# Scores kept and masked in PSUM in natural order, read permuted by the exponential

## The reference

```python
latent_kv = x @ w_kv_down              # 1024 x 128
kv = latent_kv @ w_kv_up               # k and v, 16 heads of 64
q = (x @ w_q)
att = einsum('bqhd,bkhd->bhqk', q, k) * 64 ** -0.5
att = where(causal, att, -inf); att = softmax(att, axis=-1)
y = einsum('bhqk,bkhd->bqhd', att, v) @ w_out
```

## Time and profile before

| | |
|---|---|
| Median of 3 runs | 1843.12 us (1841.56 to 1847.8) |
| The profiled execution, its own time | 1841.02 us |
| Its span | 1839.6 us |
| Busy in the span | TensorE 95%, VectorE 68%, ScalarE 49%, GpSimd 47% |
| Pair loop of the first batch, scores of the first round to the last round's | 29.3 to 235.4 us |
| Granted TensorE clock | 0.995 of full speed |

### The profile page before, as it was taken

How to read it: one execution, slowest core, us unless ns; L and a number is a source line. 1 busy time by engine, 2 the same in 40 slices (tenths; PEclk the granted TensorE clock), 3 DMA queues, 4 the chain that set the end, 5 groups by cost and what they waited for, 6 DMA issues and landing times.

```text
span 1839.6 us, 41212 instructions
## 1 busy us (share of the span) xinstructions
PE 1748.0 (95%) x16374; PEld 1237.8 (67%) x16374; DVE 1259.3 (68%) x2775; ACT 894.8 (49%) x1970; POOL 856.5 (47%) x1282
## 2 busy tenths in 40 slices
PE   7899999998999999999999999999999999999998
PEld 4666775757567677566856777756675666765667
DVE  5688857626788884862678888575367888667445
ACT  5577725133567662422357675332246667443233
POOL 2677753141177784222127777324113777731410
PEclk9899999999999999999999999999999999999999
DMA  8555540141355553032135555204014555420500
GB/s 233 121 138 141 118 149 1 21 72 36 87 133 126 127 125 119 1 54 40 36 107 129 130 125 119 106 1 85 8 37 132 128 125 129 109 92 2 92 1 25
DMA packets 119343, 163.76 MB, mean 89 GB/s; under 512 B 30224, under 2 KB 86256, under 8 KB 118128
## 3 DMA queue, kind: packets, MB, share of 16 engines
q1 hardware_dynamic: 105712, 154.83, 35.1%
q10 hardware_dynamic: 13440, 6.30, 1.2%
HBM read 62.44 MB, written 4.24 MB: 36 GB/s over the span
## 4 chain that ended last, share of the span: by engine, by line
PE 79%; DVE 9%; SPq 5%; ACT 3%; issue 1%; DMA 1%; POOL 1%; DVEq 0%; POOLq 0%
PE bank L661 13%; PE scores L641 12%; PE scores L450 12%; PE bank L450 7%; PE bank L702 5%; SPq L978 3%; PE bank L708 3%; PE bank L704 3%; PE scores L1702 2%; PE scores L1615 2%; PE scores L1086 2%; SPq L347 2%; PE scores L1143 2%; PE scores L421 1%; PE scores L1262 1%; PE bank L718 1%
## 5 line engine op out<-in xcount | busy, mean ns | idle before, releaser
L866 POOL COPY placed<-prob 32x768 f32<-32x768 f32 x384 | 316.4, 824 | 27.5
L287 POOL TENSOR_TENSOR rstd<-rstd,minus_half 128x2 f32<-128x2 f32 x96 | 69.6, 726 | 549.7 <-DVE rstd L286 548.7
L905 ACT ACTIVATE prob<-prob,neg_max 128x768 f32<-128x768 f32 (+5 forms) x384 | 273.6, 714 | 97.0 <-DVE neg_max L787 97.0
L661 PEld LDWEIGHTS bank<-placed,v_t 128*64 128x64 f32 x4608 | 252.2, 138 | 73.5 <-issue 73.5
L661 PE MATMUL bank<-placed,v_t 128*64 128x128 f32 x4608 | 275.3, 276 | 14.9 <-DMA placed<-prob 11.2
L641 PE MATMUL scores<-k_t,q_t 64*128 64x128 f32 (+10 forms) x2176 | 287.9, 410 | 0.0
L795 DVE STREAM_TRANSPOSE prob<-prob 128x1536 f32<-128x1536 f32 x128 | 223.0, 1766 | 21.0 <-ACT prob L905 20.8
L641 PEld LDWEIGHTS scores<-k_t,q_t 64*128 64x128 f32 x2176 | 165.0, 187 | 71.8 <-issue 60.2
L787 DVE CUSTOM_DVE_ANT_1 prob<-scores,hx 128x128 f32<-128x128 f32 (+4 forms) x320 | 165.3, 576 | 46.3 <-PE scores L641 44.4
L854 POOL COPY rec_wide<-rec 128x128 f32<-128x128 f32 x256 | 65.5, 291 | 245.2 <-DVE rec L799 178.3
L866 POOL COPY placed<-hx 32x768 f32<-32x768 f32 x192 | 158.1, 824 | 13.7
(11 more groups left out here) (254 smaller groups left out, 3272.6 us busy)
## 6 DMA issues: line engine op xcount, KB each, us to landing
placed<-prob SPq DMA_DIRECT2D x640, 96.0 KB, 2.2
f<-in_L_ffn_f SPq DMA_DIRECT2D x16, 2048.0 KB, 13.3
placed<-hx SPq DMA_DIRECT2D x320, 96.0 KB, 2.1
x<-in_L_attn_x SPq DMA_DIRECT2D x8, 512.0 KB, 4.4
mod_rows<-mod_scratch SPq DMA_DIRECT2D x32, 128.0 KB, 5.4
out<-x SPq DMA_DIRECT2D x16, 256.0 KB, 2.1
w_ring<-in_L_attn_w_q ACTq DMA_DIRECT2D x24, 128.0 KB, 2.4
w_ring<-in_L_attn_w_kv_up ACTq DMA_DIRECT2D x48, 64.0 KB, 2.1
```

The lines of the kernel that those rows point to most:

```text
L287: step = pool.do(lambda e, ts=ts: nc.gpsimd.tensor_tensor(rstd[:, ts], rstd[:, ts], minus_half[:, ts], op=ALU.pow), var, filled)
L661: last = nc.tensor.matmul(out_bank[rows_, at_:at_ + P], v_t[pair % 2][:, j, rows_], placed[m % 2][:, :, head, first_block(m, i) + j, :], s ...
L866: nc.gpsimd.tensor_copy(placed[m % 2][target * GROUP:(target + 1) * GROUP, source, :, :, :], prob[m % 3][source * GROUP:(source + 1) * GRO ...
L905: nc.scalar.activation(p_, p_, ACT.Exp, scale=-1.0, bias=neg_max[:, k:k + 1], accum_out=row_sum[:, k:k + 1]).then_inc(flow["exp_done"], 1)
```

## The change

Keys, scores and mask are in natural order. The score matmuls are cut at bank edges alone. VectorE masks the scores in place in PSUM, all parts of head 0 first, then those of head 1. The exponential reads PSUM in the permuted order and writes `prob`. An exponential waits for the masks of all parts of its head that have a share in its banks (last_beside), not for its own alone. TensorE's waits for the score banks go by exp_done instead of masked, and the wait for the moves goes from VectorE to ScalarE's first exponential of a round. The masks count per head (part_number), and ScalarE's order of exponentials is head by head too.

```diff
-        future = hx[:, 0:TH, :].rearrange("p t n -> p (t n)").rearrange("p (g m) -> p g m", g=GROUPS)
-        future_edge = future[:, :, (T - 1) * GROUP:]
+        future = hx[:, 0:TH, :].rearrange("p t n -> p (t n)")
+        future_edge = future[:, (T - 1) * P:]
...
-            out=future_edge, in_=future_edge, compare_op=ALU.is_ge, fill=BIG, base=0, pattern=[[-GROUP, GROUPS], [-1, GROUP]],
+            out=future_edge, in_=future_edge, compare_op=ALU.is_ge, fill=BIG, base=0, pattern=[[-1, P]],
...
-            return parts_through(m) - HEADS * (len(tiles_in(m)) - i) + head + 1
+            return parts_through(m) - len(tiles_in(m)) * (HEADS - head) + i + 1
...
         def pieces_of(m, i):
 
-            at_, width, pieces = first_block(m, i) * P, (tiles_in(m)[i] + 1) * GROUP, []
-            for g in range(GROUPS):
...
+            at_, end, key, pieces = first_block(m, i) * P, (first_block(m, i) + tiles_in(m)[i] + 1) * P, 0, []
+            while at_ < end:
+                edge = min(end, (at_ // 512 + 1) * 512)
+                pieces.append((at_, key, key + edge - at_))
+                at_, key = edge, key + edge - at_
             return pieces
+
+        def last_beside(m, i):
+
+            return max(j for j in range(len(tiles_in(m))) if first_block(m, j) // 4 <= last_bank(m, i))
...
+        def scores_of(m, i, head):
+            blocks = blocks_in(m, i)
+            return score_tiles[head][:, :, :].rearrange("p a n -> p (a n)")[:, blocks.start * P:blocks.stop * P]
...
                 if m > 0:
-                    e.wait_ge(flow["masked"], base["masked"] + parts_through(m - 1))
+                    e.wait_ge(flow["exp_done"], base["exp_done"] + parts_through(m - 1))
...
-                        last = nc.tensor.matmul(score_tiles[head][:, at_ // 512, at_ % 512:at_ % 512 + count],
+                        last = nc.tensor.matmul(score_tiles[head][:, at_ // 512, at_ % 512:at_ % 512 + hi - lo],
                                                 q_t[buf][rows_, tile * P:(tile + 1) * P],
-                                                k_of[buf][rows_, groups, lo:hi], start=True, stop=True)
+                                                k_t[buf][rows_, lo:hi], start=True, stop=True)
...
             def turn_inverse(m):
                 e.wait_ge(flow["widened"], base["widened"] + m + 1)
-                e.wait_ge(flow["masked"], base["masked"] + parts_through(min(m + 1, ROUNDS - 1)))
+                e.wait_ge(flow["exp_done"], base["exp_done"] + parts_through(min(m + 1, ROUNDS - 1)))
...
-                nc.vector.tensor_copy(keys_half(0, int(j[1])), by_group(bank_of(0, j))).then_inc(flow["job_read_dve"], 1)
+                nc.vector.tensor_copy(k_t[0][:, int(j[1]) * HW:(int(j[1]) + 1) * HW], bank_of(0, j)).then_inc(flow["job_read_dve"], 1)
...
                 nc.vector.tensor_tensor_reduce(
-                    prob[m % 3][:, :, head, blocks, :].rearrange("p g n i -> p g (n i)"),
-                    src.rearrange("p (g m) -> p g m", g=GROUPS), future[:, :, (T - 1 - tile) * GROUP:],
-                    1.0, BIG, op0=ALU.add, op1=ALU.min, accum_out=neg_max[:, k:k + 1]).then_inc(flow["masked"], 1)
+                    src, src, future[:, (T - 1 - tile) * P:], 1.0, BIG, op0=ALU.add, op1=ALU.min, accum_out=neg_max[:, k:k + 1]).then_inc(flow["masked"], 1)
...
-                e.wait_ge(flow["exp_done"], base["exp_done"] + parts_through(m) - HEADS + head + 1)
+                e.wait_ge(flow["exp_done"], base["exp_done"] + part_number(m, len(tiles_in(m)) - 1, head))
...
-                if b * ROUNDS + m > 2:
-                    moved, count = all_moved(m - 3)
-                    e.wait_ge(flow[moved], count)
-                    e.wait_ge(flow["kept"], base["kept"] + len(COPIES) * (m - 2))
...
-                for i in range(len(tiles_in(m))):
-                    for head in range(HEADS):
+                for head in range(HEADS):
+                    for i in range(len(tiles_in(m))):
                         minimum(m, i, head)
...
-                    last = nc.scalar.copy(keys_half(pair % 2, half), by_group(ps))
+                    last = nc.scalar.copy(k_t[pair % 2][:, cols], ps)
...
             def exponential(m, i, head):
-                p_ = prob[m % 3][:, :, head, blocks_in(m, i), :].rearrange("p g n i -> p g (n i)")
                 k = column_of(m, i, head)
-                e.wait_ge(flow["masked"], base["masked"] + part_number(m, i, head))
-                nc.scalar.activation(p_, p_, ACT.Exp, scale=-1.0,
+                if i == 0 and head == 0 and b * ROUNDS + m > 2:
+                    moved, count = all_moved(m - 3)
+                    e.wait_ge(flow[moved], count)
+                    e.wait_ge(flow["kept"], base["kept"] + len(COPIES) * (m - 2))
+                e.wait_ge(flow["masked"], base["masked"] + part_number(m, last_beside(m, i), head))
+                nc.scalar.activation(prob[m % 3][:, :, head, blocks_in(m, i), :],
+                                     scores_of(m, i, head).rearrange("p (n g i) -> p g n i", g=GROUPS, i=GROUP), ACT.Exp, scale=-1.0,
                                      bias=neg_max[:, k:k + 1], accum_out=row_sum[:, k:k + 1]).then_inc(flow["exp_done"], 1)
...
+                for i in range(large + 1):
+                    exponential(m, i, 0)
                 for i in range(large):
-                    for head in range(HEADS):
-                        exponential(m, i, head)
+                    exponential(m, i, 1)
                 if b == 0 and m == 1:
                     mod_read()
-                exponential(m, large, 0)
                 if m > 1 and first:
                     read_values(m - 2)
                 exponential(m, large, 1)
...
-        banks.readers = [all_of("values_read"), all_of("job_read_act")] + [all_of("masked")] * 5 + [all_of("rec_copied")]
+        banks.readers = [all_of("values_read"), all_of("job_read_act")] + [all_of("exp_done")] * 5 + [all_of("rec_copied")]
```

More of the change, by code:

```diff
@@ L563, in pieces_of @@
         def pieces_of(m, i):
-            at_, width, pieces = first_block(m, i) * P, (tiles_in(m)[i] + 1) * GROUP, []
-            for g in range(GROUPS):
[L567 to L575, removed]
-            return pieces
+            at_, end, key, pieces = first_block(m, i) * P, (first_block(m, i) + tiles_in(m)[i] + 1) * P, 0, []
[3 more added lines that the diff above has]
+                at_, key = edge, key + edge - at_
+            return pieces
+        def last_beside(m, i):
+            return max(j for j in range(len(tiles_in(m))) if first_block(m, j) // 4 <= last_bank(m, i))
         def last_bank(m, i):
             return ((first_block(m, i) + tiles_in(m)[i] + 1) * P - 1) // 512
+        def scores_of(m, i, head):
+            blocks = blocks_in(m, i)
+            return score_tiles[head][:, :, :].rearrange("p a n -> p (a n)")[:, blocks.start * P:blocks.stop * P]
         def out_slot(m, tile):
@@ L632, in scores @@
                 if m > 0:
-                    e.wait_ge(flow["masked"], base["masked"] + parts_through(m - 1))
+                    e.wait_ge(flow["exp_done"], base["exp_done"] + parts_through(m - 1))
                 pieces = [(tile,) + piece for i, tile in enumerate(tiles_in(m)) for piece in pieces_of(m, i)]
                 ends = {piece[1] // 512: piece[1] for piece in pieces}
-                for tile, at_, groups, lo, hi in pieces:
-                    count = (groups.stop - groups.start) * (hi - lo)
+                for tile, at_, lo, hi in pieces:
                     if m > 1 and at_ // 512 == SCORE_BANKS - 1:
@@ L779, in first_job @@
                 e.wait_ge(flow["job_done"], base["job_done"] + job_number(0, j))
-                nc.vector.tensor_copy(keys_half(0, int(j[1])), by_group(bank_of(0, j))).then_inc(flow["job_read_dve"], 1)
+                nc.vector.tensor_copy(k_t[0][:, int(j[1]) * HW:(int(j[1]) + 1) * HW], bank_of(0, j)).then_inc(flow["job_read_dve"], 1)
             def minimum(m, i, head):
-                tile, blocks = tiles_in(m)[i], blocks_in(m, i)
+                tile, src = tiles_in(m)[i], scores_of(m, i, head)
                 k = column_of(m, i, head)
-                src = score_tiles[head][:, :, :].rearrange("p a n -> p (a n)")[:, blocks.start * P:blocks.stop * P]
                 e.wait_ge(flow["scores_done"], base["scores_done"] + HEADS * (SCORE_BANKS * m + last_bank(m, i)) + head + 1)
                 nc.vector.tensor_tensor_reduce(
-                    prob[m % 3][:, :, head, blocks, :].rearrange("p g n i -> p g (n i)"),
-                    src.rearrange("p (g m) -> p g m", g=GROUPS), future[:, :, (T - 1 - tile) * GROUP:],
-                    1.0, BIG, op0=ALU.add, op1=ALU.min, accum_out=neg_max[:, k:k + 1]).then_inc(flow["masked"], 1)
+                    src, src, future[:, (T - 1 - tile) * P:], 1.0, BIG, op0=ALU.add, op1=ALU.min, accum_out=neg_max[:, k:k + 1]).then_inc(flow["masked"], 1)
             def shuffle(m, head):
```

(2 more changed lines are left out.)

## The result

The changed kernel takes 1874.24 us (median of 4 runs, 1873.11 to 1875.37) against 1842.34 for the kernel before in the same series: a ratio of 1.0174, 95% interval 1.0155 to 1.0193. That is +31.9 us, where +36.7 was forecast, and the time lies in the range. The span of the profiled execution went from 1839.6 to 1871.4 us.

The account below looks back on a forecast made before the run. TensorE was taken to bound the pair loop (25.48 us a pair); the new wait for exponentials adds 28.1 + 7.0 + 5.6 - 4 = +36.7 us, forecast 1880 us by the runs' median, range 1861 to 1902.

Parts of the forecast that it names:

- B: Pair-loop round of tiles 3 and 7: head order ends the last exponential later, so it lasts 8.19 us, +0.29.
- C: Pair-loop round of tiles 4 and 6: first exponential waits for both masks of its head; 9.00 us, +0.96.
- A: Pair-loop round of tiles 0, 2, 1, 5: TensorE's work covers the wait; fewer matmul records give about -0.08 us.
- unknown (1): ScalarE's exponential from PSUM, permuted: -0.02 us each, seven on a pair's path, -4 us over the kernel.
- inner pairs: Six in each of four batches, three rounds each: +1.17 us a pair, +28.1 us in all.
- the rival in which PSUM can't be read and written at once: VectorE's mask in place runs at half rate and VectorE becomes the bound: +196 us, 2040; 4%.
- First pairs: First pair of each batch, no values so short rounds: the wait for exponentials shows more, +7.0 us.
- Last pairs: Last pair of each of four batches, no jobs to cover the wait: +5.6 us.
- the wait is covered: Exponentials from PSUM 0.16 us shorter, rounds end inside TensorE's work, only fewer matmuls count: -14 us, 1829; 3%.
- The larger pieces: Score matmuls cut at bank edges alone, fewer records: -0.44 us a pair over 32 pairs, -14 us.

Follow-up runs that it names:

- fine_waits: The changed kernel with each score bank waiting for its own exponentials only, inverses turned into head 0's bank, copy_rec ahead of the second job's copy: 1856.63 us.
- order_wait: The kernel before with masks and exponentials head by head and TensorE waiting for exp_done, exponentials still reading SBUF: 1861.93 us.

## Why the prediction was right, point by point

- **B, +0.29**: +0.20. **C, +0.96**: +0.75. **A, -0.08**: -0.13. (The forecast figures are those ahead of unknown (1), which takes 0.02 off each of seven exponentials: +0.23 and +0.88 for B and C with it. The inner pairs then come to 24.7 us forecast and 18.7 measured.) The chain was the one that bounds B, and one of two that bound C; its start in C was forecast to 0.03 us, and the experiments reproduce its parts: 0.46 a pair for order and wait, as expected before that run (B 0.29, C 0.17; measured 0.25 and 0.21), 0.82 for the neighbour's mask.
- **What was too large was a size, that of unknown (1)**, the exponential from PSUM at -0.02 us. The groups by shape in the changed kernel, against 1150 and 715 ns before:

```profile
L894 ACT ACTIVATE prob<-scores,neg_max 128x1024 f32<-128x1024 f32 x64 | 71.8, 1123 | 44.3 <-DVE neg_max L779 44.3
...
L894 ACT ACTIVATE prob<-scores,neg_max 128x512 f32<-128x512 f32 x64 | 43.7, 683 | 44.9 <-DVE neg_max L779 43.3 <-DMA placed<-prob 1.6
```

  The durations are 0.027 and 0.032 shorter, and issue to issue it is up to 0.06 (0.66 in place of 0.72 for 512: 131.61 to 132.27, and the earlier trace rows). Four on C's chain make most of the missing 0.2. By the Trainium skill (VectorE: DVE Perf Modes, the section on the TRN2 errata) a PSUM source saves ScalarE 52 cycles at 1.2 GHz, which makes 43 ns as an estimate. That lies between the two readings, and was the better price. The same section of the Trainium skill gives VectorE 62 cycles more for a PSUM source and states nothing for an output there. This case has the output: the large mask went from 1.22 to 1.25 us and its accumulator read from 0.083 to 0.143, so ScalarE starts 0.05 later behind it (129.18 to 130.50 is 1.32, where it was 1.27), while VectorE's next mask still starts 1.15 us behind the one before.

```profile
129.18 1.23 DVE L779 CUSTOM_DVE_ANT_0 scores<-scores,hx 128x1024 f32<-128x1024 f32 x1 [0.96 <-PE scores L634]
130.33 0.14 DVE L779 DVE_READ_ACCUMULATOR2_ANT neg_max<- 128x1 f32 x1
...
130.50 1.12 ACT L894 ACTIVATE prob<-scores,neg_max 128x1024 f32<-128x1024 f32 x1 [1.39 <-DVE neg_max L779]
```

  That also answers the rival in which PSUM can't be read and written at once: a mask of 1024 elements in place takes 1.25 us, not twice 1.22.
- **First pairs, +7.0**: +8.2. A went to 7.71 (forecast 7.99), B to 7.94 (7.93), C to 8.79 (9.00). **Last pairs, +5.6**: +7.6 less 1.2. A went to 8.09, not 8.56: I had left read_values on its chain, 0.26 us, where in the last pair it comes behind the last exponential (688.17 behind 687.30), and the exponentials were shorter. What made both sums larger nevertheless is a thing that I had not priced, the clock (below): 1.5 us in one first pair and 3.4 in two last pairs. Without these 4.9 us the last pairs would come to 3.1 against 5.6, and the whole to 27 against 36.7. So it is in part luck that the total came within 5 us of the forecast.
- **The v job behind read_values** was missing from the prediction's sum for C. It cost nothing on top there, because it ended with the exponentials. But it is a second reason for C's length, as fine_waits shows: with the exponentials' wait out of the way C still took 8.71 us. The rival "the wait is covered" had only the first reason in it.
- **The larger pieces**, -0.44 a pair in that rival: measured alone they gave 6.6 us, not 14, because the moves come next.

## What to carry to other kernels

When a buffer's reader is replaced by a later one, write down the chain from the producer to the new reader for each stage, with the order in which the engines take their parts: here the wait alone cost 6 us, the new order alone 3, both 20, and a wait for a neighbour in the same bank 24 more. Look for the second chain that ends at the same time before relieving the first; two of them tied here, and relieving one showed nothing or little. And before counting a saving on the bounding engine, ask what hands it its next input: with the larger pieces alone, half of the expected saving was missing, and TensorE waited longer for the moves.

## What the runs showed of the hardware

TensorE's granted clock sometimes fell to the lower of its two levels (1.2 of 2.4 GHz) behind a pause of about 2 us, and sometimes did not behind the same pause. In the changed kernel's last pairs TensorE stands still for 2.12 us ahead of the turn before B; in two of the four batches the scores of B then took 4.54 us in place of 2.85, at a mean granted clock of 0.62, and in the other two, after the same pause, 2.85:

```profile
1148.66 0.41 PE L665 MATMUL scores<-ident,rec_wide 128*128 128x128 f32 x2 [2.12 <-issue]
1148.99 2.85 PE L634 MATMUL scores<-k_t,q_t 64*128 64x512 f32 x12
...
1610.31 0.41 PE L665 MATMUL scores<-ident,rec_wide 128*128 128x128 f32 x2 [2.12 <-issue]
1610.64 4.54 PE L634 MATMUL scores<-k_t,q_t 64*128 64x512 f32 x12
```

Ahead of round C of the first pairs of three batches it stands still for 2.62 us; the clock fell behind one of these pauses (scores 3.93 us in place of 2.86). Busy time and clock of such stretches in the changed kernel:

```profile
1610.64:1615.18 4.54, 4.54 (x15) 1.75 (x16) 2.22 (x4) 1.15 (x3) 3.44 (x8) 0.62 0.59 136
1434.87:1438.80 3.93, 3.93 (x19) 1.88 (x20) 1.77 (x4) 0.59 (x1) 2.61 (x5) 0.72 0.56 127
```

In order_wait, behind a pause of 2.60 us, the scores of C in a first pair took 5.85 us where they take 3.15, at 0.53:

```profile
514.15:520.00 5.85, 5.85 (x31) 3.75 (x32) 1.73 (x4) 1.30 (x2) 4.46 (x7) 0.53 0.60 138
```

The kernel before has such stretches too, outside the pair loops: behind a pause of 1.73 us its clock is 0.50 from 894.90 to 897.80, and behind an equal pause 1.00 from 442.98 to 445.90. So a stall on the bounding engine can cost more than its own length, here 1.1 to 2.7 us on top. It also varies between executions of one kernel: the profiled one of order_wait shows a mean granted clock of 0.990 and took 1868.89 us, its other three show 0.994 to 0.995 and took 1860.8 to 1862.19. Why some pauses were spared stays open.
